# Two score slots and one probability slot in PSUM instead of three slots in rotation

## Chip, cores and metric

The kernel runs on one core of one Trainium2 chip. The metric is device time in microseconds, of the whole launch. Before the change three runs gave 754.0 us in the median (752.06 to 757.2).

## The reference

Input `x` is 4 batches of 1024 tokens with 128 channels. Cut to what matters, the computation for each batch is

```
k_eff, v_eff = products of W_dq, W_uq, W_uk, W_uv, W_o      # per head, 16 heads of 8 channels
c_kv  = x @ W_dkv.T ;  q = x @ W_dq.T @ W_uq.T
attn  = softmax(causal(q_lat @ c_kv.T / sqrt(8)))           # 1024 x 1024, 16 heads
y     = (attn @ c_kv) @ v_eff
x     = layernorm(x + y)
gate, up = fp4_linear(x, w_gate), fp4_linear(x, w_up)       # 128 -> 352, FP4 in blocks of 16
x     = layernorm(x + fp4_linear(silu(gate) * up, w_down))  # 352 -> 128
```

All in float32. The softmax subtracts the maximum of each query's row, and the kernel computes this maximum exactly, in a pass of its own.

## The kernel before, in words

**Tiling.** The heads go in four quads of four heads (`QUADS`), each quad in 18 steps (`STEPS`), so a batch has 72 steps (`BODY`) and the four batches 288. In each step TensorE computes two tiles of 128 x 1024 float32, each of which takes two banks of PSUM.

- A *score tile* S (`score_max`, lines 511 to 524) has queries on partitions. VectorE reads it for the maximum over the keys (`maximum`, line 837). It runs 24 steps (`STEPS + LEAD`) ahead of the other pass, and the first 24 tiles are made in a prologue. The maxima are combined after a quad's 18 tiles (line 846), split into three bf16 parts by GpSimd (`top_split`, lines 1080 to 1088), transposed by TensorE (`mt`, line 461), copied by ScalarE (line 686), and written by SyncE's DMAs as three more rows into the query operand (line 371).
- A *probability tile* T (`score_probs`, lines 526 to 542) has keys on partitions and subtracts the maximum through these rows. ScalarE reads it with one exp (`exps`, line 715) into `probs`, a ring of six buffers in SBUF.

Twelve times in 18 steps (`W_STEP`) TensorE multiplies finished probabilities by the values (`weigh`, line 556, called W here). Tiles that cross the causal diagonal get their mask as small matmuls (line 507).

**Where a tile lies.** PSUM has eight banks: `ring[0]` to `ring[2]` are three slots of two banks, `yt_ps` and `misc` one bank each. In the main loop the order of tiles S(0), T(0), S(1), T(1) and so on goes round the three slots: S(n) lies in slot 2n mod 3, T(n) in slot (2n+1) mod 3.

**What TensorE waits for.** Step n on TensorE is S(n), the jobs of the step, T(n), then W if there is one, in this order. S(n) overwrites the slot of T(n-2), so it waits for exp n-2. T(n) overwrites the slot of S(n-1), so it waits for the maximum of S(n-1). In the prologue S(s) waits for the maximum of S(s-3). In the last 24 steps of the last batch there are no more score tiles, and T goes round all three slots alone.

**The order of everything else** is written out by hand in `jobs` and in the tables `H_A`, `H_V`, `H_P`, `LN_AT`: for each step, which pieces of the projections, of the first norm and of the previous batch's feed-forward part run on which engine (`misc_job` on TensorE, `misc_read` and `sigmoid` on ScalarE, and so on). Each engine runs its own list in order. ScalarE's list for a step is its reads of `misc`, then the sigmoid of the feed-forward part (lines 722 and 724, behind GpSimd's clamp, line 1151), then the exp. After the last batch a tail does the feed-forward part of batch 3.

Of the kernel before, what the change touches and what calls it, by code (L numbers as in the profile page):

```python
# [30 lines left out]
LEAD = 6  # L31
STEPS = 18
P_RING = 6
# [16 lines left out]
def build(nc, x, w_dq, w_uq, w_dkv, w_uk, w_uv, w_o, w_gate, w_up, w_down, out):  # L50
    B, T, C = x.shape
# [96 lines left out]
    with ExitStack() as ctx:  # L148
# [168 lines left out]

        block = ctx.enter_context(nc.Block())

        def tile_pos(b, a, s):  # L320

            u = a + s // STEPS
            return b + u // QUADS, u % QUADS, s % STEPS
# [93 lines left out]
        def _(pe):  # L417
# [93 lines left out]
            def score_max(b, a, s, slot):  # L511

                if s == 0:
                    pe.wait_ge(op_in[a].sem, op_in[a].at(b, 3))
                for i, kc, p, at, n in S_LIST[s]:
                    pair = PAIRS * a + p
                    diag = kc == i // PER
                    for e in range(2):
                        lo = HALF * e
                        last = nc.tensor.matmul(ring[slot][:, e, at:at + n], q_op[lo:lo + ROWS, pair, i * P:(i + 1) * P],  # L520
                                                k_op[lo:lo + ROWS, pair, kc * CHUNK:kc * CHUNK + n], start=True, stop=not diag)
                    if diag:
                        last = causal(slot, at + n - P, mask_s)
                last.then_inc(s_mm.sem, 1)
# [53 lines left out]
                    nc.tensor.transpose(misc[0:w, 0:P], wd[:, f * P:f * P + w], ident[:, :]).then_inc(prep_mm.sem, 1)  # L578

            for s in range(STEPS + LEAD):  # L580
                if s >= 3:
                    pe.wait_ge(s_max.sem, s - 2)
                score_max(0, s // STEPS, s % STEPS, s % 3)
                if 4 <= s < 4 + 3 * FT:
                    weight_t(s - 4)
                if s == STEPS + 1:
                    pe.wait_ge(prep_cp.sem, 4 + 3 * FT)
                    misc_job("mt", 0, 0)
# [3 lines left out]
            for b in range(B + 1):  # L592
                if b == B:

                    pe.wait_ge(t_exp.sem, t_exp.at(B - 1, BODY - 1))
                for n in range(BODY):
                    if b < B:
                        a, s = n // STEPS, n % STEPS
                        nb, na, ns = tile_pos(b, a, s + STEPS + LEAD)
                        if nb < B:  # L600
                            if n < 2 and b == 0:
                                pe.wait_ge(s_max.sem, STEPS + LEAD)
                            else:
                                pn = b * BODY + n - 2
                                pe.wait_ge(t_exp.sem, pn + 1)
                            score_max(nb, na, ns, 2 * n % 3)
                    for job in jobs_at(b, n):
                        misc_job(*job)
                    if b < B:

                        if nb < B:
                            pe.wait_ge(s_max.sem, b * BODY + n + STEPS + LEAD)
                        else:
                            pe.wait_ge(s_max.sem, B * BODY)
                            pe.wait_ge(t_exp.sem, b * BODY + n - 2)
                        score_probs(b, a, s, (2 * n + 1) % 3)

                    for w, at in enumerate(W_STEP):
                        g = n - at
                        if g % STEPS == 0 and g >= 0 and b < B:  # L620
                            weigh(b, g // STEPS, w)
                        elif g % STEPS == 0 and g < 0 and b > 0:
                            weigh(b - 1, QUADS - 1, w)
# [3 lines left out]
        def _(act):  # L627
# [79 lines left out]
            def exps(b, a, s):  # L707

                n = STEPS * a + s
                act.wait_ge(t_mm.sem, t_mm.at(b, n))  # L710
                g = b * BODY + n - P_RING
                if g >= 0:

                    act.wait_ge(av_mm.sem, g // STEPS * WS + FREED[g % STEPS])
                nc.scalar.activation(probs[:, n % P_RING, :, :], ring[(2 * n + 1) % 3][:, :, :],  # L715
                                     ACT.Exp, scale=SCALE).then_inc(t_exp.sem, 1)

            def sigmoid(b, t):
# [76 lines left out]
        def _(dve):  # L795
# [34 lines left out]
            def maximum(b, a, s, slot):  # L830

                g = b * BODY + STEPS * a + s
                dve.wait_ge(s_mm.sem, g + 1)
                if s == 0 and g > 0:
                    dve.wait_ge(m_all.sem, b * QUADS + a)
                for i, kc, p, at, n in S_LIST[s]:
                    last = nc.vector.tensor_reduce(top[:, kc, :, p, i], ring[slot][:, :, at:at + n], AX.X, ALU.max)  # L837
                last.then_inc(s_max.sem, 1)
# [20 lines left out]
            dve.wait_ge(wq_v.sem, 3)  # L859
            nc.vector.tensor_scalar(w_b[:, :, :], w_b[:, :, :], 1.0, ROUND, ALU.max, ALU.mult).then_inc(wq_v.sem, 1)  # L860
            for s in range(STEPS + LEAD):
                maximum(0, s // STEPS, s % STEPS, s % 3)
                if s == STEPS - 1:
                    combine(0, 0)

# [122 lines left out]
            for b in range(B + 1):  # L988
                for n in range(BODY):
                    a, s = n // STEPS, n % STEPS  # L990
                    if b < B:
                        nb, na, ns = tile_pos(b, a, s + STEPS + LEAD)
                        if nb < B:
                            maximum(nb, na, ns, 2 * n % 3)
                            if ns == STEPS - 1:
                                combine(nb, na)
                    for kind, jb, k in jobs_at(b, n):
                        if kind == "k":
                            k_range(jb, k)
                        elif kind == "q":  # L1000
                            part_rest(jb, 2 + k)
                        elif kind == "yn":
                            output(jb, k)
                        elif kind == "up":
                            up_product(jb, k)
                        elif kind == "down" and k % 2:
                            second_sum(jb, k // 2)
                    if n in K_REST_AT and b + 1 < B:
                        part_rest(b + 1, K_REST_AT.index(n))
                    for nb, c, stage in first_norm_at(b, n):  # L1010
                        if stage == 0:
                            norm_stats(nb, c)
                        elif stage == 1:
                            first_norm(nb, c)
                        else:
                            quant_x(nb, c, stage - 2)
                    if b > 0:
                        for stage, t in tile_at(b, n, H_V if b < B else TAIL_H_V):
                            quant_h(b - 1, t, stage)
                        for c, stage in second_norm_at(b, n):  # L1020
                            (second_stats, last_norm)[stage](b - 1, c)
# [198 lines left out]
```

## Time and profile before

| | |
|---|---|
| median of 3 runs | 754.0 us (752.06 to 757.2) |
| profiled execution, its own time | 758.44 us |
| its span, first to last instruction | 756.6 us |
| TensorE matmul busy | 563.6 us (74%), 5863 instructions |
| VectorE busy | 532.3 us (70%), 981 |
| ScalarE busy | 412.3 us (54%), 598 |
| GpSimd busy | 316.0 us (42%), 441 |
| mean granted TensorE clock | 0.876 of full speed |

PE is TensorE's matmul, PEld its weight load, DVE VectorE, ACT ScalarE, POOL GpSimd, SPq SyncE's queue. A wait is the idle time of an engine ahead of an instruction, and the arrow names what released it. Busy time of an engine is a share over a prologue, a main loop and a tail that have different limits.

### The profile page before, as it was taken

What the parts mean: (1) busy time and instruction counts of PE and PEld (TensorE: products, weight loads), DVE (VectorE), ACT (ScalarE), POOL (GpSimd) and SP (SyncE); (2) the same over time, 40 slices, a digit from 0 to 9 for tenths busy, and PEclk for the clock granted to TensorE, in tenths of its full rate; (3) what the DMA queues carried; (4) which work ended last, traced back from release to release, by engine and by line L of the source; (5) the groups of instructions that cost most, each with busy time, mean ns of one, the idle gap of its engine ahead of it and who ended that gap; (6) DMA issues with size and microseconds to landing.
All of it is one profiled execution on the core that took longest, in us unless ns stands there. A gap on an engine that the chain in (4) does not pass through costs nothing.

```text
span 756.6 us, 15168 instructions
## 1 busy us (share of the span) xinstructions
PE 563.6 (74%) x5863; PEld 254.3 (34%) x5863; DVE 532.3 (70%) x981; ACT 412.3 (54%) x598; POOL 316.0 (42%) x441
## 2 busy tenths in 40 slices
PE   4275988589787888788888889696978897862623
PEld 2132333233333434333333334242323342421412
DVE  0389787388889767788788778888787784264461
ACT  2311766377665766565576666564656675742220
POOL 4520032000436654433337464533273536258682
PEclk9655999799998999999898999998899998995565
DMA  3393006602300192020300480203000000000000
GB/s 101 77 241 101 2 3 151 145 2 51 94 5 12 31 210 56 15 52 16 92 16 2 90 196 11 56 10 78 3 16 3 3 2 16 1 15 0 0 14 15
DMA packets 34222, 37.91 MB, mean 50 GB/s; under 512 B 6390, under 2 KB 19766, under 8 KB 34150
## 3 DMA queue, kind: packets, MB, share of 16 engines
q1 hardware_dynamic: 33238, 36.39, 20.0%
q8 instruction: 47, 0.77, 0.4%
q10 hardware_dynamic: 912, 0.54, 0.3%
q14 instruction: 25, 0.20, 0.1%
HBM read 19.64 MB, written 16.78 MB: 48 GB/s over the span
## 4 chain that ended last, share of the span: by engine, by line
PE 39%; DVE 31%; POOL 13%; issue 10%; ACT 4%; DMA 2%; SPq 1%; POOLq 0%; DVEq 0%; ACTq 0%
DVE top L837 19%; PE yt_ps L556 11%; PE ring L537 6%; PE ring L520 5%; PE misc L495 3%; PE ring L507 2%; PE misc L466 2%; POOL eg L1151 2%; POOL hx L1123 2%; POOL hx L1121 2%; POOL hx L1125 1%; DVE z L906 1%; PE misc L455 1%; PE misc L486 1%; DVE hc L963 1%
## 5 line engine op out<-in xcount | busy, mean ns | idle before, releaser
L837 DVE TENSOR_REDUCE top<-ring 128x2 f32<-128x1024 f32 (+3 forms) x384 | 349.6, 948 | 113.4 <-PE ring L507 80.2
L715 ACT ACTIVATE probs<-ring 128x1024 f32<-128x1024 f32 x288 | 293.8, 1027 | 132.1 <-PE ring L507 79.7
L556 PE MATMUL yt_ps<-probs,v_op 128*32 128x512 f32 (+3 forms) x1536 | 171.6, 520 | 0.5 <-ACT probs L715 0.5
L537 PE MATMUL ring<-q_op,k_op 59*128 59x512 bf16 (+3 forms) x768 | 124.0, 346 | 50.2 <-DVE top L837 40.3
L520 PE MATMUL ring<-k_op,q_op 56*128 56x512 f16 (+3 forms) x768 | 127.8, 355 | 44.5 <-ACT probs L715 18.9
L520 PEld LDWEIGHTS ring<-k_op,q_op 56*128 56x128 bf16 x768 | 38.4, 96 | 171.0 <-issue 116.8
L1144 POOL TENSOR_TENSOR r<-r,yq 128x128 f32<-128x128 f32 x32 | 14.6, 457 | 168.3 <-DVE yq L876 168.3
L537 PEld LDWEIGHTS ring<-q_op,k_op 59*128 59x128 f16 x768 | 37.7, 95 | 120.8 <-DVE top L837 58.7
L507 PE MATMUL ring<-ident,mask_s 64*128 64x64 bf16 x1024 | 59.5, 198 | 0.0
L507 PEld LDWEIGHTS ring<-ident,mask_s 64*128 64x128 bf16 x1024 | 47.7, 102 | 17.7 <-issue 5.0
L507 PEld LDWEIGHTS ring<-ident,mask_t 64*128 64x128 bf16 x1024 | 47.2, 100 | 18.2 <-issue 6.8
L507 PE MATMUL ring<-ident,mask_t 64*128 64x64 bf16 x1024 | 52.0, 196 | 0.0
L1151 POOL TENSOR_SCALAR eg<-eg 128x352 f32<-128x352 f32 x32 | 35.1, 1098 | 28.0 <-ACT eg L698 27.6
L722 ACT ACTIVATE eg<-eg,one 128x352 f32<-128x352 f32 x32 | 18.7, 586 | 41.0 <-POOL eg L1151 41.0
L556 PEld LDWEIGHTS yt_ps<-probs,v_op 128*32 128x32 f32 x1536 | 30.9, 110 | 29.6 <-issue 18.5
L1121 POOL TENSOR_TENSOR hx<-hx,hc 128x352 f32<-128x352 f32 x32 | 29.8, 931 | 20.7 <-DVE hc L966 20.7
L486 PE MATMUL ring<-ident,hx 128*128 128x128 f32 (+1 forms) x24 | 6.7, 414 | 42.6 <-POOL hx L1125 42.6
L1080 POOL TENSOR_SCALAR top_parts<-top_all 128x32 bf16<-128x32 f32 x16 | 4.8, 297 | 68.3 <-DVE top_all L846 68.2
L1123 POOL TENSOR_TENSOR hx<-hx,hc 128x352 f32<-128x352 f32 x32 | 29.8, 930 | 2.5
L1155 POOL TENSOR_TENSOR h<-gu,eg 128x352 f32<-128x352 f32 x32 | 29.8, 930 | 0.0
L963 DVE TENSOR_SCALAR hc<-hx 128x352 uint32<-128x352 uint32 x32 | 15.8, 492 | 16.3 <-POOL hx L1160 16.3
L1125 POOL TENSOR_TENSOR hx<-hx,h_sc 128x352 f32<-128x352 f32 x32 | 25.2, 787 | 2.5
(170 smaller groups left out, 758.4 us busy)
## 6 DMA issues: line engine op xcount, KB each, us to landing
q_op<-scratch_q SPq DMA_DIRECT2D x32, 224.0 KB
k_op<-scratch_k SPq DMA_DIRECT2D x32, 224.0 KB
scratch_k<-k_part SPq DMA_DIRECT2D x32, 192.0 KB, 3.3
scratch_q<-q_part SPq DMA_DIRECT2D x32, 128.0 KB, 3.1
scratch_q<-q_part SPq DMA_DIRECT2D x16, 192.0 KB, 3.3
xp<-in_L_attn_x_dram SPq DMA_DIRECT2D x4, 512.0 KB, 4.4
r<-in_L_attn_x_dram SPq DMA_DIRECT2D x8, 256.0 KB, 2.8
out_dram<-z SPq DMA_DIRECT2D x8, 256.0 KB, 2.3
```

Source lines behind the costliest of these rows:

```text
L507: last = nc.tensor.matmul(ring[slot][:, e, at + HALF * half:at + HALF * (half + 1)], mask[group, half, :], ident16[group, group], start=Fa ...
L520: last = nc.tensor.matmul(ring[slot][:, e, at:at + n], q_op[lo:lo + ROWS, pair, i * P:(i + 1) * P], k_op[lo:lo + ROWS, pair, kc * CHUNK:kc ...
L537: last = nc.tensor.matmul(ring[slot][:, e, at:at + n], k_op[lo:lo + rows, pair, j * P:(j + 1) * P], q_op[lo:lo + rows, pair, (c + 1) * CHU ...
L556: last = nc.tensor.matmul(yt_ps[32 * q:32 * (q + 1), lo:CHUNK], v_op[:, j, 4 * a + q, :], probs[:, (STEPS * a + tile) % P_RING, q % 2, at: ...
L715: nc.scalar.activation(probs[:, n % P_RING, :, :], ring[(2 * n + 1) % 3][:, :, :], ACT.Exp, scale=SCALE).then_inc(t_exp.sem, 1)
L837: last = nc.vector.tensor_reduce(top[:, kc, :, p, i], ring[slot][:, :, at:at + n], AX.X, ALU.max)
L963: nc.vector.tensor_scalar(hc[:, n, :, :].bitcast(U32), hx[:, n, :, :].bitcast(U32), 0x7F800000, None, ALU.bitwise_and).then_inc(he_v.sem, 1)
L1121: nc.gpsimd.tensor_tensor(dst, dst, magic, ALU.add).then_inc(s1.sem, 1)
L1123: nc.gpsimd.tensor_tensor(dst, dst, magic, ALU.subtract).then_inc(s2.sem, 1)
L1125: nc.gpsimd.tensor_tensor(dst, dst, sc_, ALU.mult).then_inc(s3.sem, 1)
L1151: nc.gpsimd.tensor_scalar(eg[:, n, :], eg[:, n, :], EXP_TOP, None, ALU.min).then_inc(e_p.sem, 1)
L1155: nc.gpsimd.tensor_tensor(hn.rearrange("p n k -> p (n k)"), gu[:, n, :], eg[:, n, :], ALU.mult).then_inc(h_p.sem, 1)
```

## The change

The slots get fixed owners. In the main loop score tiles take slots 0 and 1 in turn (n mod 2), and probability tiles always take slot 2, up to the last 24 steps, where T goes round all three as before. The waits follow: S(n) waits for the maximum of S(n-2), T(n) for exp n-1. In the prologue score tiles also use two slots, so S(s) waits for the maximum of S(s-2). No operation on data is added, removed or moved in any engine's order.

```diff
@@ -317,6 +317,10 @@
 
         block = ctx.enter_context(nc.Block())
 
+        def probs_slot(m):
+
+            return 2 if m < B * BODY - STEPS - LEAD else m % 3
+
         def tile_pos(b, a, s):
 
             u = a + s // STEPS
@@ -578,9 +582,9 @@
                     nc.tensor.transpose(misc[0:w, 0:P], wd[:, f * P:f * P + w], ident[:, :]).then_inc(prep_mm.sem, 1)
 
             for s in range(STEPS + LEAD):
-                if s >= 3:
-                    pe.wait_ge(s_max.sem, s - 2)
-                score_max(0, s // STEPS, s % STEPS, s % 3)
+                if s >= 2:
+                    pe.wait_ge(s_max.sem, s - 1)
+                score_max(0, s // STEPS, s % STEPS, s % 2)
                 if 4 <= s < 4 + 3 * FT:
                     weight_t(s - 4)
                 if s == STEPS + 1:
@@ -598,22 +602,19 @@
                         a, s = n // STEPS, n % STEPS
                         nb, na, ns = tile_pos(b, a, s + STEPS + LEAD)
                         if nb < B:
-                            if n < 2 and b == 0:
-                                pe.wait_ge(s_max.sem, STEPS + LEAD)
-                            else:
-                                pn = b * BODY + n - 2
-                                pe.wait_ge(t_exp.sem, pn + 1)
-                            score_max(nb, na, ns, 2 * n % 3)
+                            pe.wait_ge(s_max.sem, b * BODY + n + STEPS + LEAD - 1)
+                            score_max(nb, na, ns, n % 2)
                     for job in jobs_at(b, n):
                         misc_job(*job)
                     if b < B:
 
                         if nb < B:
-                            pe.wait_ge(s_max.sem, b * BODY + n + STEPS + LEAD)
+                            if b * BODY + n > 0:
+                                pe.wait_ge(t_exp.sem, b * BODY + n)
                         else:
                             pe.wait_ge(s_max.sem, B * BODY)
                             pe.wait_ge(t_exp.sem, b * BODY + n - 2)
-                        score_probs(b, a, s, (2 * n + 1) % 3)
+                        score_probs(b, a, s, probs_slot(b * BODY + n))
 
                     for w, at in enumerate(W_STEP):
                         g = n - at
@@ -712,7 +713,7 @@
                 if g >= 0:
 
                     act.wait_ge(av_mm.sem, g // STEPS * WS + FREED[g % STEPS])
-                nc.scalar.activation(probs[:, n % P_RING, :, :], ring[(2 * n + 1) % 3][:, :, :],
+                nc.scalar.activation(probs[:, n % P_RING, :, :], ring[probs_slot(b * BODY + n)][:, :, :],
                                      ACT.Exp, scale=SCALE).then_inc(t_exp.sem, 1)
 
             def sigmoid(b, t):
@@ -859,7 +860,7 @@
             dve.wait_ge(wq_v.sem, 3)
             nc.vector.tensor_scalar(w_b[:, :, :], w_b[:, :, :], 1.0, ROUND, ALU.max, ALU.mult).then_inc(wq_v.sem, 1)
             for s in range(STEPS + LEAD):
-                maximum(0, s // STEPS, s % STEPS, s % 3)
+                maximum(0, s // STEPS, s % STEPS, s % 2)
                 if s == STEPS - 1:
                     combine(0, 0)
 
@@ -991,7 +992,7 @@
                     if b < B:
                         nb, na, ns = tile_pos(b, a, s + STEPS + LEAD)
                         if nb < B:
-                            maximum(nb, na, ns, 2 * n % 3)
+                            maximum(nb, na, ns, n % 2)
                             if ns == STEPS - 1:
                                 combine(nb, na)
                     for kind, jb, k in jobs_at(b, n):
```

## Rows read from the trace of the kernel before

**Rows 1.** The page: the chain that ended last, by engine.

```profile
PE 39%; DVE 31%; POOL 13%; issue 10%; ACT 4%; DMA 2%; SPq 1%; POOLq 0%; DVEq 0%; ACTq 0%
```

**Rows 2.** Busy us by stretch, then granted clock and DMA share.

```profile
72.00:630.00 558.00, 463.80 (x5187) 200.52 (x5187) 443.27 (x785) 351.05 (x479) 217.57 (x313) 0.94 0.21 49
...
666.00:757.00 91.00, 35.89 (x140) 23.72 (x132) 41.25 (x106) 21.34 (x52) 54.86 (x62) 0.60 0.03 9
```

**Rows 3.** TensorE waits, 72 to 630 us: line, releaser, total us, times, longest.

```profile
PE ring L537 <- DVE top L837: 40.3, 47, 2.6
PE ring L520 <- ACT probs L715: 18.9, 13, 2.4
...
PE misc L451 <- DVE gu L939: 7.7, 6, 3.0
PE misc L474 <- DVE yq L876: 3.1, 3, 1.2
PE misc L461 <- POOL top_parts L1088: 2.9, 9, 0.5
PE misc L455 <- DVE rest L828: 2.7, 4, 1.0
PE misc L480 <- DVE yq L876: 1.7, 3, 0.6
PE misc L486 <- POOL hx L1125: 1.4, 5, 0.3
PE misc L495 <- DVE gu L939: 1.1, 3, 0.4
```

**Rows 4.** Waits of VectorE, 72 to 630 us.

```profile
DVE top L837 <- PE ring L507: 72.0, 64, 9.8
DVE top L837 <- PE ring L520: 31.7, 40, 2.7
```

**Rows 5.** Waits of ScalarE, 72 to 630 us.

```profile
ACT eg L722 <- POOL eg L1151: 19.6, 11, 3.1
```

**Rows 6.** Line 715: count, ns min/median/max, first and last start, 72 to 630 us.

```profile
L715 ACT ACTIVATE probs<-ring x264: 1003/1024/1061, 71.7 to 628.5; 128x1024 f32<-128x1024 f32 x132
```

**Rows 7.** Line 537, 72 to 630 us, the same columns.

```profile
L537 PE MATMUL ring<-q_op,k_op x702: 216/376/631, 72.5 to 629.5; 59*128 59x512 bf16 x89, 59*128 59x128 bf16 x58, 59*128 59x256 bf16 x29
```

**Rows 8.** TensorE timeline: start, us, operation, [idle before <- releaser], 311 to 334 us.

```profile
311.95 0.39 PE L537 MATMUL ring<-q_op,k_op 59*128 59x512 bf16 x2
...
315.72 0.39 PE L537 MATMUL ring<-q_op,k_op 59*128 59x512 bf16 x2
...
318.58 0.28 PE L520 MATMUL ring<-k_op,q_op 56*128 56x256 f16 x2 [2.41 <-ACT probs L715]
...
330.05 0.39 PE L537 MATMUL ring<-q_op,k_op 59*128 59x512 bf16 x2 [1.08 <-DVE top L837]
...
333.17 0.34 PE L537 MATMUL ring<-q_op,k_op 59*128 59x384 bf16 x2
```

**Rows 9.** ScalarE timeline, 311 to 337 us.

```profile
312.38 1.02 ACT L715 ACTIVATE probs<-ring 128x1024 f32<-128x1024 f32 x1 [1.08 <-PE ring L537]
...
317.52 1.01 ACT L715 ACTIVATE probs<-ring 128x1024 f32<-128x1024 f32 x1
...
328.21 1.02 ACT L715 ACTIVATE probs<-ring 128x1024 f32<-128x1024 f32 x1 [0.56 <-PE ring L507]
...
332.42 1.02 ACT L715 ACTIVATE probs<-ring 128x1024 f32<-128x1024 f32 x1
```

**Rows 10.** Timeline of the prologue, 40 to 75 us.

```profile
41.58 20.85 DVE L837 TENSOR_REDUCE top<-ring 128x2 f32<-128x1024 f32 x24 [7.65 <-PE ring L507]
...
65.24 3.75 SPq L371 DMA_DIRECT2D q_op<-top_t  x6
...
70.54 0.61 PE L520 MATMUL ring<-k_op,q_op 56*128 56x512 f16 x2 [2.88 <-DVE top L837]
```

**Rows 11.** DMA issues, 60 to 75 us: count, KB each, median us to landing.

```profile
q_op<-top_t SPq DMA_DIRECT2D x6, 4.0 KB, 1.7
```

## What the change will do to the time

> **What bounds the kernel now.** I read the busy time by stretch first [rows 2]. After a prologue comes the main loop, and from 666 us on a tail that has no S or T tile. Between 72 and 630 us, where both kinds of tile run, TensorE is busy for 463.8 of 558 us (83%), VectorE for 443.3 (79%), ScalarE for 351.1 (63%). So TensorE is the spine of the loop, with VectorE close behind, and the chain that ended last says the same: PE 39%, DVE 31%, ACT 4% [rows 1]. No engine is full. What counts is therefore how TensorE's idle time, 94.2 us = 558 - 463.8, is made up.
>
> The waits of TensorE in this stretch give the answer [rows 3]. T tiles waited 40.3 us for VectorE's maximum (47 times), S tiles 18.9 us for the exp (13 times), and the jobs in `misc` waited for other work, 20.6 us over the seven rows shown (7.7 + 3.1 + 2.9 + 2.7 + 1.7 + 1.4 + 1.1). The first two, 59.2 us, are exactly the waits for a free slot that the change takes away. VectorE in turn waited 103.7 us (72.0 + 31.7) for score tiles [rows 4], so it could take them earlier: it doesn't stop a gain by itself.
>
> **What the change takes away.** T(n) no longer waits for the maximum of S(n-1). S(n) no longer waits for exp n-2. At most 59.2 us come back. The new wait of S(n), for the maximum of S(n-2), lies one tile of VectorE's work earlier than what T(n) waited for, and TensorE has T and W in between, so I cost it at nothing. What hides it is VectorE being done by then. That cover shrinks when TensorE gets ahead, and the price if it goes is in the rivals.
>
> **What it adds.** T(n) now waits for exp n-1, which is the reader of the tile just before it. The chain T, exp, T has one slot and can't overlap with itself. Its floor comes from two rows: T starts at 311.95 [rows 8], its exp at 312.38 and takes 1.02 us [rows 9], so it ends 1.45 us after the T started. From the end of a releaser to the matmul it releases there are 0.05 to 0.06 us (exp 317.52 + 1.01 = 318.53, S tile 318.58). The floor is 1.51 us from T to T, and somewhat more for a masked T. The mean interval of the loop is 555.6 / 262 = 2.12 us, well above it. But the intervals are very uneven, since W and the jobs come in some steps only: the waiting T has W(n-1), S(n) and the jobs of n as its cover, and without W and job that is one S tile. Behind the waiting T on TensorE's queue are W(n), S(n+1) and all later jobs; for W and for S waits VectorE and `yt_ps`, so a late T delays everything but the exp itself.
>
> **How I worked out the sum.** There are 264 exps in the loop, the first at 71.7 and the last at 628.5 us [rows 6], and T matmuls from 72.5 to 629.5 us [rows 7]. For each of the 262 intervals from the second T to the 264th I took the old length, subtracted the idle time that a removed wait had caused in it, and compared this with the time from the T's start to its exp's end, plus 0.06. The larger is the new length. Where the exp was late only since ScalarE had a backlog from the exp before, I counted ScalarE's own work between the two exps instead. That is because a T that waits for the exp before it lets no backlog of exps build up. Three examples:
> - T at 330.05 waited 1.08 us for VectorE [rows 8]. The exp before it ended at 328.21 + 1.02 = 329.23 [rows 9]. The T moves up to 329.29, so 0.76 us come back, not 1.08.
> - T at 333.17 had no wait [rows 8]. The exp before it ends at 332.42 + 1.02 = 333.44 [rows 9]. The T moves back to 333.50: 0.33 us lost.
> - T at 315.72 had no wait [rows 8]. The exp before it ended only at 318.53 [rows 9], since ScalarE stood behind a sigmoid that waited for GpSimd's clamp: such waits are 19.6 us, 11 times, in the loop [rows 5]. The T moves to 318.59, 2.87 us later. But the S tile at 318.58 had waited 2.41 us for that same exp [rows 8], and that wait goes. What stays is the T tile's own time, which used to run beside the stall: about 0.4 us. So most of the 18.9 us of S waits is no gain. The stall moves one tile up.
>
> For two quads in full: from 287.2 us the changes are +0.48, +0.33, +0.14, +0.32, +0.02, +2.86 - 2.48, +0.14, together +1.8 us. The next one, from 327.7 us, has more waits for VectorE: -0.02, -0.76, +0.33, +0.08, -0.32, +0.38, +0.32, +1.01, -0.20, -0.72, -0.66, -0.16, together -0.7 us. Over all 262 intervals 103 get longer by 45.5 us and 39 shorter by 33.5 us. **The main loop's term is +12.0 us.**
>
> The other terms: the last 24 steps keep their waits (T for exp n-3) and the tail has no ring at all, 0. In the prologue VectorE runs without a pause, 18 tiles in 24 instructions and 20.85 us, 1.16 us a tile, while a score tile without a mask takes TensorE 0.61 us (70.54) [rows 10]. So the second slot is filled while VectorE reads the first. The first S tile of the main loop may start one tile earlier than at 70.54, which is worth at most 1.2 us to VectorE. T(0) behind it gains almost nothing, since its maximum rows come from six DMAs whose issue ends at 65.24 + 3.75 = 68.99, plus 1.7 to landing [rows 11]: 70.7. I take 0, with bounds of -1.2 and, for a maximum that now and then finds its tile late, +2.
>
> Sum: 0 + 12 + 0 = +12 on the profiled execution's 758.4, so 770. The median of the runs is 754.0, 4.4 us under the profiled execution. I carry the difference over and get 766. The sum leaves two corrections of opposite sign open (the jobs' waits, which can swallow delays, and gains that VectorE doesn't let through). The first seems to me a little surer, as each job wait lies right behind some T: I take 2 us off. **764 us**, 1.3% slower.
>
> A page of the Trainium skill speaks against this change outright: Perfetto Trace Analysis, section Matmuls, wants independent matmul groups to rotate through different PSUM banks so that the reading of one overlaps the next group's matmuls, and the T tiles stop doing so. The rows bear this out in part only, as 159 of the 262 intervals (262 - 103) don't get longer. Taken as a rule without exception it would keep the losses and none of the gains, 754 + 45.5 = 799; that is the far end of the second rival.
>
> **The rivals.**
> 1. *The delays are swallowed (faster).* The jobs of a step sit right behind a late T or just ahead of the next one, and they waited 20.6 us in the rows for VectorE and GpSimd [rows 3]. A T that comes late ahead of such a job costs nothing. If all of it is swallowed, and the prologue's 1.2 us come too: 12 - 20.6 - 1.2 = -9.8, so 744 us. It decides from the point where more than 12 of these 20.6 us fall into intervals that got longer. For it: 59.2 us of slot waits go for certain, and VectorE has 103.7 us in which it waits for TensorE [rows 4]. Against it: the job waits are few (the 7.7 us are six waits), and 103 delays are spread over all steps.
> 2. *The lockstep costs more (clearly slower).* The gains of 33.5 us need S(n+1) to go out early, and it now waits for the maximum of S(n-1) in its turn. VectorE is 79% busy. If half of the gains stay with VectorE: 12 + 16.8 = 29, so 783 us. If none comes: 799. For it: in the quad from 327.7 us the T waits for VectorE follow each other closely. Against it: VectorE's idle time.
> 3. *It evens out (no change).* The 59.2 us of removed waits meet new waits of the same size, with half of the job waits swallowed: 12 - 10.3 = +1.7, so 756 us.
> 4. *It stays on paper.* If TensorE were the bound at nearly every step, neither wait would matter. Its 94.2 us of idle time speak against that, so I give it no chance of its own and put it into the third.
>
> **How the numbers follow.** Forecast (758 to 772 us) 0.41, second rival 0.16, third 0.22, first 0.21. A measurement of this kernel tells about 1% from no change, 746.5 to 761.5 us. The first rival's chance goes to faster, 0.20, with the little that is left near the edge. Of the forecast's own chance some 0.07 lies below 761.5, so same is 0.30, and slower 0.50. The range takes in rival 1's price and rival 2's half price: 743 to 784. Outside it remain a swallowing larger than the rows show, and the upper end of rival 2.
>
> **What would show it in the changed profile.**
> - TensorE's wait of line 537 for VectorE (40.3 us now) gone, and in its place one for ScalarE's exp, of some 50 to 60 us.
> - Its wait of line 520 for the exp (18.9) gone. A new one of line 520 for VectorE below 10 us would confirm my zero for it, and one of 20 or more would be rival 2.
> - No interval from T to T under 1.5 us. At the step where ScalarE waits for GpSimd's clamp the stall of 2.4 us stands ahead of the T, not of the S.
> - VectorE's waits for score tiles up by about 10 us, with its busy time the same.
> - Job waits on TensorE: near 20 us by my sum, near 0 by rival 1.
>
> I'm wrong if the exp has more cover than its end times say, if the order of work on ScalarE comes out differently once T tiles are late, or if a late T makes a maximum late and through it the chain of max, split, transpose and DMA that opens each quad: that would come 15 times, and nothing above prices it.

## The result: 3.0% slower

| | before | changed |
|---|---|---|
| median | 755.6 us (4 runs) | 779.0 us (4 runs) |
| ratio | | 1.030 [1.026, 1.034] |
| profiled execution, its span | 758.4, 756.6 us | 778.2, 776.4 us |
| T(1) to T(263) | 555.6 us | 576.3 us |

The forecast was slower, 764 us; measured is 779. The direction was right, the amount less than half of what came: +10 forecast, +23.4 measured. 779 lies within the range and near the half price of the second rival (783). Two executions took twice the usual time, 1733 us in e1 and 1563 us in one of the kernel before, and are left out of every comparison.

Of the changed kernel first the chain by engine and the busy time by stretch, with the columns of [rows 1, 2]. The loop ends 20 us later, so the stretches do too.

```profile
PE 40%; DVE 19%; ACT 14%; POOL 12%; issue 10%; DMA 2%; SPq 1%; POOLq 0%; ACTq 0%; DVEq 0%
```

```profile
72.00:650.00 578.00, 472.42 (x5177) 201.82 (x5177) 440.90 (x784) 353.66 (x478) 216.82 (x312) 0.93 0.20 47
...
686.00:777.00 91.00, 35.50 (x136) 23.83 (x132) 40.23 (x106) 21.19 (x52) 54.53 (x62) 0.62 0.03 9
```

ScalarE's share of the chain went from 4% to 14%, VectorE's from 31% to 19%. All of the loss lies in the main loop. Prologue and tail are the same. In this stretch TensorE idles for 105.6 us (578 - 472.4) in place of 94.2, and is busy for 472.4 us in place of 463.8. The sum had no term for the second; the section on the prediction takes it up. Now its waits in the loop, as in [rows 3], then VectorE's and ScalarE's, as in [rows 4, 5].

```profile
PE ring L541 <- ACT probs L716: 68.6, 96, 2.8
PE ring L541 <- issue: 9.7, 2, 7.9
PE ring L524 <- DVE top L838: 6.6, 4, 3.1
PE misc L455 <- DVE gu L940: 5.5, 6, 1.9
PE misc L459 <- DVE rest L829: 3.4, 6, 0.6
PE misc L478 <- DVE yq L877: 3.2, 3, 1.1
PE misc L465 <- POOL top_parts L1089: 2.2, 5, 1.2
PE ring L541 <- DVE top L838: 1.1, 1, 1.1
```

```profile
DVE top L838 <- PE ring L511: 86.3, 69, 8.8
DVE top L838 <- PE ring L524: 39.9, 40, 2.6
```

```profile
ACT eg L723 <- POOL eg L1152: 21.3, 11, 3.1
```

Line 541 is T (537 before), line 524 is S (520), line 716 the exp, line 838 the maximum. The waits of 40.3 and 18.9 us are gone. T waits 68.6 us for the exp, 96 times. VectorE waits 126.2 us for score tiles (86.3 + 39.9), where it waited 103.7.

The three examples of the prediction can be read in two views of the changed kernel, TensorE's timeline and ScalarE's:

```profile
328.51 0.39 PE L541 MATMUL ring<-q_op,k_op 59*128 59x512 bf16 x2 [2.79 <-ACT probs L716]
...
339.34 0.39 PE L541 MATMUL ring<-q_op,k_op 59*128 59x512 bf16 x2 [0.32 <-ACT probs L716]
...
342.79 0.34 PE L541 MATMUL ring<-q_op,k_op 59*128 59x384 bf16 x2 [0.26 <-ACT probs L716]
...
347.73 0.39 PE L541 MATMUL ring<-q_op,k_op 59*128 59x512 bf16 x2
...
349.24 0.39 PE L541 MATMUL ring<-q_op,k_op 59*128 59x512 bf16 x2 [0.44 <-ACT probs L716]
```

```profile
326.43 0.59 ACT L723 ACTIVATE eg<-eg,one 128x352 f32<-128x352 f32 x1 [3.08 <-POOL eg L1152]
...
327.45 1.01 ACT L716 ACTIVATE probs<-ring 128x1024 f32<-128x1024 f32 x1
```

The T at 315.72 in [rows 8] is now at 328.51, behind the sigmoid's stall and the exp that ends at 328.46. The T at 330.05 there waits 0.32 us in place of 1.08, now for the exp. The T at 333.17, which didn't wait, waits 0.26. From 347.73 to 349.24 one sees the floor, 1.51 us. Over the loop no interval is shorter than 1.50 us; before, 60 were under it.

### The profile page after: what moved, and what is told of

The parts are those of the page before. It is cut to its first block, busy times and chain, and to the rows that moved or that the text cites. A ratio compares the mean times of both kernels' runs of the same rounds, so it can differ in the third digit from the quotient of the medians.

```text
span 776.4 us, 15168 instructions
## 1 busy us (share of the span) xinstructions
PE 572.4 (74%) x5863; PEld 255.5 (33%) x5863; DVE 530.2 (68%) x981; ACT 415.6 (54%) x598; POOL 315.3 (41%) x441
## 3 DMA queue, kind: packets, MB, share of 16 engines
q1 hardware_dynamic: 33238, 36.39, 19.6%
## 4 chain that ended last, share of the span: by engine, by line
PE 40%; DVE 19%; ACT 14%; POOL 12%; issue 10%; DMA 2%; SPq 1%; POOLq 0%; ACTq 0%; DVEq 0%
PE yt_ps L560 13%; DVE top L838 10%; ACT probs L716 10%; PE ring L541 8%; PE ring L524 5%; PE misc L499 3%; POOL eg L1152 3%; PE ring L511 3%; PE misc L484 1%; DVE z L907 1%; POOL hx L1124 1%; POOL hx L1122 1%; ACT yt L732 1%; ACT eg L723 1%; PE misc L490 1%
## 5 line engine op out<-in xcount | busy, mean ns | idle before, releaser
L541 PE MATMUL ring<-q_op,k_op 59*128 59x512 bf16 (+3 forms) x768 | 124.9, 348 | 81.1 <-ACT probs L716 68.6
L560 PE MATMUL yt_ps<-probs,v_op 128*32 128x512 f32 (+3 forms) x1536 | 173.9, 526 | 0.5 <-ACT probs L716 0.5
L524 PE MATMUL ring<-k_op,q_op 56*128 56x512 f16 (+3 forms) x768 | 129.7, 359 | 31.8 <-DMA k_op<-scratch_k 18.0
```

What stands on the lines that cost most here:

```text
L541: last = nc.tensor.matmul(ring[slot][:, e, at:at + n], k_op[lo:lo + rows, pair, j * P:(j + 1) * P], q_op[lo:lo + rows, pair, (c + 1) * CHU ...
L560: last = nc.tensor.matmul(yt_ps[32 * q:32 * (q + 1), lo:CHUNK], v_op[:, j, 4 * a + q, :], probs[:, (STEPS * a + tile) % P_RING, q % 2, at: ...
```

## The experiments

Two theories were left after the result. **Lockstep**: the loss is T's wait for the exp of the tile before it. **VectorE**: VectorE holds back the S tiles, which now have two slots, and with them the gains. And one question: what the removed waits gave back. Ratios are to the kernel before, with their 95% intervals.

**A short maximum (e1, e2, e11).**

```
-  nc.vector.tensor_reduce(top[...], ring[slot][:, :, at:at + n], AX.X, ALU.max)
+  nc.vector.tensor_reduce(top[...], ring[slot][:, :, at:at + n // 8], AX.X, ALU.max)
```

The exp's scale is also multiplied by 0.01 here, in this pair and in e12, so that nothing overflows. The length of the exp stays at 1.03 us.

> The kernel before, with VectorE's row maximum over an eighth of each tile's columns (and the exp's scale times 0.01, so that nothing overflows; both change the values). Theory: before the change the T tiles wait 40.3 us for VectorE; with a short maximum that wait falls below 3 us and TensorE gets most of it back, so 715 to 735 us. Rival (VectorE's load limits both kernels alike, and the change lost by what S tiles wait for VectorE): the same fall here, and an equal one in the changed kernel.

> The changed kernel with the same short maximum. Theory: its loss is T waiting for the exp of the tile before, which VectorE has no part in. So T's wait for ScalarE stays at 60 us or more, S's wait for VectorE goes from 6.6 to 0, and the time falls by 5 to 12 us only, to 767 to 774: the distance to the kernel before grows from 23 to 40 us or more. Rival (the gains are held back by VectorE): it falls by 30 or more, and the distance stays at 23 or shrinks.

> The same kernel as e1, for a profile of an undisturbed execution: 700 to 704 us, T's wait for VectorE below 3 us, TensorE busy above 85% between 72 and 600 us.

Measured: before with it 702.7 us, 0.929 [0.925, 0.933]; changed with it 744.0 us, 0.986 [0.983, 0.989]. e11 is e1's kernel again, for its trace; its one run gave 705.9 us. The distance grows from 23 to 41 us, with VectorE busy for 278 us in place of 532 (e11, whole span). TensorE's waits for slots, first in e11, then in e2 (72 to 650 us):

```profile
PE ring L520 <- ACT probs L715: 16.7, 15, 2.2
PE ring L537 <- DVE top L837: 6.0, 5, 2.7
```

```profile
PE ring L541 <- ACT probs L716: 61.6, 100, 1.8
```

T's wait for the exp stays at 61.6 us when VectorE is quick, and the distance grows, so VectorE is not what makes the changed kernel slower than the other. But I had the changed kernel falling by 5 to 12 us, and it fell by 35, which was one of the two marks that I had set for the rival. So VectorE's length counts there too, although its rows have few waits for the maximum (6.6 and 1.1 us). Of the 30 us between T(1) and T(263), 19.3 are idle time of TensorE and 10.8 busy time with the same matmuls (472.0 to 461.2), and its clock was at the lower level for 52 us there in place of 76. What of VectorE's work sets the pace, no run here separates.

**A short exp (e3, e4).**

```
-  nc.scalar.activation(probs[:, n % P_RING, :, :], ring[...][:, :, :], ACT.Exp, ...)
+  w = CHUNK if b == 0 and n < P_RING else CHUNK // 2
+  nc.scalar.activation(probs[:, n % P_RING, :, 0:w], ring[...][:, :, 0:w], ACT.Exp, ...)
```

> The kernel before, with the exp over half of each tile's columns, from the seventh tile on (the other half of the probabilities stays as it was). Exp from 1.03 to about 0.6 us. Theory: T's wait for VectorE stays at about 40 us and S's wait for the exp falls little, since it comes from the clamp of the feed-forward part: 745 to 754 us. Rival: ScalarE's length counts before too, below 740.

> The changed kernel with the same short exp. Theory: the floor from T to T falls from 1.51 to about 1.08 us, so T's wait for the exp falls from 68.6 to 20 to 30 us (what stays is the clamp's stall), and the kernel is level with the one before with the same exp or up to 20 us faster: 730 to 755 us. Rival (something else in the fixed slots costs, whatever the exp's length): it stays 15 us or more slower than the kernel before with the same exp.

Measured: before with it 748.7 us, 0.991 [0.988, 0.995]; changed with it 749.2 us, 0.993 [0.990, 0.996]. **The 3% is gone.** In e4 the exp takes 0.60 us, T's wait for it is 35.6 us and S's wait for VectorE 12.5 us (72 to 650 us):

```profile
PE ring L541 <- ACT probs L717: 35.6, 48, 2.4
PE ring L524 <- DVE top L839: 12.5, 14, 3.2
```

The shortest interval there is 1.075 us, as the floor less 0.43 says. The exp's length is what makes the fixed slots slow. Note the second row, though: with the exp out of the way, S waits for VectorE about twice as long as in the changed kernel (6.6 us). The fixed slots are level with the rotation and not faster.

**The new wait alone (e5, e17), and the price of a second semaphore (e16, e18).** e5 and e17 are one kernel, the one before with

```
+  if nb < B and b * BODY + n > 0:
+      pe.wait_ge(t_exp.sem, b * BODY + n)
   score_probs(b, a, s, (2 * n + 1) % 3)
```

> The kernel before with its three slots in rotation, and one more wait: T(n) also waits for exp n-1, which no slot asks for. It has the changed kernel's new wait and keeps the two old ones, so it splits the change: up to here it's what the new wait costs, and from here to the changed kernel what the removed waits give back. Worked out interval by interval from the trace of before, as in the prediction but with T's waits for VectorE kept: +28.6 us, so 780 to 786 us, 3 to 10 us slower than the changed kernel. Rival (the slots' places in PSUM or the two-slot prologue cost something, not the wait): close to 754.

Measured 786.6 us, 1.040 [1.036, 1.044]. On the face of it the new wait costs 30 us and the removed ones give back 7.6. But its trace has 263 instructions more, the second waits. A T that waits for the exp comes 0.14 us after the exp's end, not 0.055, and the shortest interval is 1.59 us, not 1.50. The experiment had a cost of its own. The same kernel with the short maximum on top, where T's wait for VectorE is down to 4.6 us, shows it:

> The kernel with rotation and T's extra wait for exp n-1 (as the kernel of both waits), with the row maximum over an eighth of the columns and the exp's scale times 0.01. With a short maximum VectorE holds no T tile back, so the two waits that the change removes are worth nothing, and the fixed slots give nothing back: within 4 us of the changed kernel with the short maximum, 740 to 748 us. If it is 8 or more slower, the fixed slots give back something that isn't a wait for VectorE.

Measured 753.7 us, 0.998 [0.995, 1.001], where the changed kernel had 744.0 with the short maximum: 10 us more. So I ran controls. In the first the changed kernel gets a second wait that is always fulfilled (`pe.wait_ge(s_max.sem, b * BODY + n + STEPS + LEAD - 1)` ahead of the one for the exp), in the last the kernel before does (`pe.wait_ge(t_exp.sem, b * BODY + n - 1)`).

> The changed kernel, whose T tile also waits once more for the maximum of S(n-2), which its own S(n) has waited for already: a wait that is always fulfilled. It's the control for the kernel of both waits: there a T tile waits for two semaphores, and in its trace the T comes 0.10 us after the exp's end in place of 0.055, with a shortest interval of 1.59 us in place of 1.50. If the second wait by itself costs that 0.05 to 0.09 us at each of some 110 T tiles that wait, this kernel is 5 to 10 us slower than the changed one, 784 to 789, and level with both waits: then the removed waits give back nothing, and the new wait alone costs about 20. If it stays at 779, the new wait costs 30 and the removed ones give back 7.

> The kernel of both waits, for a comparison on the same chip with the spare wait: 783 to 788 us. The difference to the spare wait's kernel is what the removed waits are worth, with the number of waits on each T equal.

> The kernel before, whose T tile also waits for exp n-2, which its own S(n) has waited for already. A second wait that is always fulfilled: it should cost only where T is the tile that TensorE gets stuck at, 47 times, so 0 to 5 us: 754 to 760. If it costs 8 or more, two semaphores on a matmul slow the stream everywhere.

The 0.10 us in the text on e16 is a misreading: in e5's trace, of which it speaks, 112 of 113 such tiles have 0.14 to 0.15 us, and in e16 114 of 115 have 0.143. The 0.09 us of the intervals is right.

| | us | ratio |
|---|---|---|
| changed kernel | 779.0 | 1.030 [1.026, 1.034] |
| changed, spare wait (e16) | 786.8 | 1.040 [1.036, 1.044] |
| both waits (e17) | 785.9 | 1.039 [1.035, 1.042] |
| before, spare wait (e18) | 755.3 | 0.999 [0.996, 1.001] |

e16 and e17 have the same number of waits on each T. e17 has the two old slot waits, and e16 doesn't; they also differ in the slots themselves and in the prologue's two or three. They are level: on one chip e17 is 0.9 us faster, each ratio known to 0.4%. **The removed waits give back nothing that can be measured**, which here means less than about 4 us. In the traces, between T(1) and T(263), TensorE idles for some 2 us less in e16 (110.2, against 112.5 in e17) and is busy for 5 us more (472.3, against 467.2). The second wait costs the changed kernel 1.0%, some 8 us. The 4% of e17 less this 1% leaves the whole 3% to the new wait; that is a difference of two runs, not a run of its own.

In e18 the second wait costs nothing, although T tiles are waited for there too: 51 of them start 0.056 us after the maximum's end, as before (0.057). The traces show what differs. In the kernels with two waits (e5, e16, e17, e18) T's first weight load carries the wait for the maximum, and the wait for the exp is an instruction of its own ahead of it. The T tiles of e17 that the maximum released start 0.057 us behind it (14 of them), those that the exp released 0.143 us behind it (116). So what costs is that the wait that ends last is the separate instruction. e16's exp and the T behind it:

```profile
287.04 1.02 ACT L717 ACTIVATE probs<-ring 128x1024 f32<-128x1024 f32 x1 [1.08 <-PE ring L541]
...
288.21 0.39 PE L541 MATMUL ring<-q_op,k_op 59*128 59x512 bf16 x2 [0.93 <-ACT probs L717]
```

TensorE's waits for VectorE and ScalarE in e17 show why little comes back (72 to 650 us):

```profile
PE ring L537 <- ACT probs L717: 75.0, 107, 2.9
PE ring L537 <- DVE top L839: 11.8, 14, 1.6
```

The waits for the maximum are all still in force here, and yet they are 11.8 us in place of 40.3. The wait for the exp comes first and VectorE catches up behind it.

**The sigmoid one step later (e6, e7).** `H_A = (2,)` becomes `H_A = (3,)`.

> The kernel before, with ScalarE's sigmoid of the feed-forward part one step later in its list (H_A from 2 to 3), so that the exp of the step goes ahead of it and doesn't stand behind GpSimd's clamp. S's wait for the exp (18.9 us) falls below 5, ScalarE's wait for the clamp (19.6) below 8: 740 to 750 us. Rival (the stall moves on, to the jobs that need the product behind the sigmoid): within 4 us of 754.

> The changed kernel with the same later sigmoid. Its stall of 2.4 to 2.9 us stands ahead of T, eight times. T's wait for the exp falls from 68.6 to 45 to 52 us and the time from 779 by 8 to 16 us, to 763 to 771. The distance to the kernel before with the same edit stays at 18 to 24, since by the prediction's sum the stall only changed its place. If the distance falls below 12, the stall was a good part of what the change costs.

Measured: before with it 760.0 us, 1.005 [1.003, 1.007]; changed with it 773.3 us, 1.023 [1.021, 1.026]. I was wrong on the first: S's wait for the exp fell to 4.9 us as expected, and the kernel got slower. The time went into the job behind it (e6, 72 to 650 us):

```profile
PE misc L486 <- POOL hx L1125: 17.5, 6, 3.2
...
PE ring L520 <- ACT probs L715: 4.9, 9, 1.2
```

Before, that job waited 1.4 us for GpSimd [rows 3]. The S tile's wait had run beside GpSimd's work. In the changed kernel T's wait for the exp fell by 19 us, to 49.3, and the kernel got only 6 us faster, since the same job waits there too (e7, 72 to 650 us):

```profile
PE ring L541 <- ACT probs L716: 49.3, 86, 1.6
PE misc L490 <- POOL hx L1126: 14.7, 7, 2.9
```

The distance is 13 us, so the edit brings the two kernels closer by 10 us. My sum had 3.7 us for the stall (+16.5 and -12.8 at steps 13 and 14). The 10 us are no measure of it, as some 4 of them are what the kernel before lost by the edit; the 6 us of the changed kernel are nearer.

**One slot for S, two for T (e8).** `probs_slot` returns `1 + m % 2`, `score_max` uses slot 0, the prologue three slots, and the waits follow.

> The mirror of the change: score tiles in one slot and probability tiles in two, in turn (the prologue with three slots, as before the change). S(n) then waits for the maximum of S(n-1), T(n) for exp n-2. In the trace of before 164 of 264 S tiles start before that maximum ends, by 128 us together, with VectorE's other work between two maxima. Much worse than the change, then: 820 to 870 us. Rival (two slots for T are worth more than two for S): below 779.

Measured 807.2 us, 1.068 [1.065, 1.072]. That is less than the 820 to 870 that I said, but the worst of the three ways to share the slots. S waits where T waited (72 to 650 us):

```profile
PE ring L524 <- DVE top L838: 102.0, 144, 1.8
```

**Slots by a plan (e9, e10).** Both use one function that keeps the occupant of each slot and waits for that occupant's reader; a list `OTHER` names the tiles that don't take the oldest slot.

```
+  for m in range(B * BODY):
+      for kind in ("ST" if m < BUSY else "T"):
+          k = order[OTHER.get((kind, m), 0)]
+          order.remove(k)
+          order.append(k)
+          SLOT[kind, m], HELD[kind, m] = k, held[k]
+          held[k] = (kind, m)
```

> The kernel before, except that in eleven quads the S tile of step 14 takes the slot of the S tile of step 13 in place of the slot of the T tile of step 12, whose exp is the one that stands behind the clamp. T of step 14 takes that one. S's wait for the exp falls from 18.9 us to below 5 and T's wait for it appears with 5 to 12 us. About -6 us: 745 to 751. Rival (as in the later sigmoid, the stall moves on with nothing gained): within 2 us of the kernel before.

> Three slots, each tile taking the one whose reader ended first in the trace of before: 30 T tiles take the slot of the last T, 14 S tiles that of another than the oldest tile, all others the oldest as before. So it has the changed kernel's removed waits where they were real and its new wait almost nowhere. T's wait for VectorE falls from 40 to 10 us or less, S's wait for the exp to below 5, T's wait for the exp stays below 15. If the removed waits come back in full where no lockstep takes them: about -16 us, 736 to 742. If VectorE holds them back (the S tile behind waits for the same maximum in its place): -6 to -9, 745 to 749, and S's wait for VectorE goes up to 8 us or more.

Measured: e9 753.4 us, 0.995 [0.992, 0.998]; e10 754.0 us, 0.994 [0.991, 0.998], 12 runs each. In e9 S's wait for the exp fell from 18.9 to 3.2 us, and the job's wait for `hx` rose from 1.4 to 13.4. Both are faster than the kernel before by half a percent by their ratios, 4 us, not by the 16 that the removed waits would be worth. In e10 (72 to 650 us):

```profile
PE ring L558 <- DVE top L850: 18.6, 32, 1.9
PE misc L507 <- POOL hx L1138: 13.5, 7, 3.2
...
PE ring L541 <- DVE top L850: 8.6, 15, 1.0
...
PE ring L558 <- ACT probs L728: 7.2, 14, 0.9
PE misc L482 <- POOL top_parts L1101: 5.7, 10, 2.0
PE ring L541 <- ACT probs L728: 4.9, 8, 1.0
```

Waits for a slot are 39.3 us (18.6 + 8.6 + 7.2 + 4.9) in place of 59.2. The job waits for `hx` and `top_parts` are 19.2 in place of 4.3. So 20 us went and 15 came back one instruction later. In the timeline it is plain. Where S waited 2.41 us for the exp before [rows 8], e10 has

```profile
316.35 0.28 PE L541 MATMUL ring<-k_op,q_op 56*128 56x256 f16 x2 [0.69 <-DVE top L850]
...
318.86 0.87 PE L507 MATMUL misc<-ident,hx 128*128 128x128 f32 x3 [2.00 <-POOL hx L1138]
```

**The job behind the removed wait, one step later (e13, e14, e15).** `(20 + 6 * t, "ht", -1, t)` becomes `(21 + 6 * t, ...)`.

> The kernel before, with the transposition of the feed-forward part's quantized tile (ht) one step later in all lists, 21 + 6t in place of 20 + 6t. Before the change the S tile of step 14 waits 2.4 us for an exp just ahead of that job, which so finds its input ready (1.4 us of waits in all). One step later it is ready all the more: within 3 us of 754. Rival (the feed-forward chain itself is late): 745 or less, or 760 and more.

> The planned slots with ht one step later. There the job's wait for GpSimd was 13.5 us, where it was 1.4 before: it took over the time of the S tile's removed wait. If that was what swallowed the gain, its wait falls below 6 us and the time by 4 to 9 us, to 743 to 749. If it doesn't fall, the removed waits were no time at all at these places, since GpSimd's and VectorE's own chain sets the pace.

> The changed kernel with ht one step later. There the stall for the clamp stands ahead of T of step 13, so ht finds its input ready (0 in the waits): within 3 us of 779. It is the control for the planned kernel: if it gets faster by 4 us or more, the later ht is good by itself.

Measured: before with it 785.1 us, 1.043 [1.039, 1.047]; planned 786.4 us, 1.044 [1.040, 1.048]; changed 817.3 us, 1.085 [1.081, 1.089]. All three lose about 4 to 5%, so the test failed as a test of where the 15 us went. The new place costs by itself: the job now waits for the read of `misc` by the job before it, and ScalarE, ahead of its exp, for the job (e13, 72 to 640 us, TensorE, then ScalarE).

```profile
PE misc L486 <- DVE yq L876: 20.4, 12, 2.7
```

```profile
ACT h_t L704 <- PE misc L486: 38.0, 20, 3.5
```

Planned slots and rotation are level here (786.4 and 785.1 us).

## Why the prediction had the direction and not the size

**The floor: right.** 1.51 us from T to T was forecast, 1.50 is the shortest interval and 1.51 the plain one. I had 103 longer intervals, and 105 got longer (by more than 0.05 us). T's wait for the exp was forecast at 50 to 60 us and is 68.6. The short exp shows that the exp's length, and through it this wait, is the cause of the 3%.

**The prologue: right.** T(0) starts 0.7 us earlier, against 0 with bounds of -1.2 and +2.

**The stall at step 13: moved as forecast, priced slightly low.** The intervals of steps 13 and 14 changed by +16.5 and -11.6 us, where the sum had +16.5 and -12.8: 4.9 us net, not 3.7. Taking most of the stall away gave the changed kernel 6 us (e7).

**The main loop's term: this step failed.** The sum had +12.0 us, and T(1) to T(263) took 20.8 us longer. 105 intervals got longer by 61.9 us and 57 shorter by 41.4, where the sum had 45.5 and 33.5. Two steps of it were wrong.

*TensorE's own time was put at no change, without a reason.* The sum says that an interval less the idle time of a removed wait is what TensorE needs. Here are the busy times between T(1) and T(263), before and changed, with the columns of [rows 2]. Both kernels run the same 5173 matmuls in the same order.

```profile
72.47:628.05 555.59, 462.63 (x5173) 200.03 (x5175) 440.89 (x781) 349.56 (x478) 217.38 (x312) 0.94 0.21 48
```

```profile
72.05:648.40 576.35, 471.91 (x5173) 201.63 (x5175) 439.28 (x780) 352.63 (x477) 216.82 (x312) 0.93 0.20 47
```

Idle time grew by 11.5 us (92.96 to 104.44), against the sum's +12.0. The other 9.3 us are busy time (462.63 to 471.91). Compared matmul by matmul they come in three parts. 4450 matmuls ran at the full clock in both kernels. Their own durations add up to nearly the same (1472.5 and 1473.7 us), but they overlap less, as TensorE starts from idle 165 times in place of 132: 4.3 us. The matmuls that ran at the lower level (1.2 GHz) in one of the kernels only add 3.9 us net, those at the lower level in both 1.0. The clock was at that level for 62.4 us of this stretch before and for 76.1 us in the changed kernel. One interval shows it, T(158) to T(159), with no wait in either kernel, first before (from 394.36 to 397.10), then changed (from 405.78 to 410.84). In the changed kernel TensorE had just stood 1.56 us for the exp ahead of T(157), and the clock was at its lower level from 404.2 to 411.0 us:

```profile
394.73 1.06 PE L556 MATMUL yt_ps<-probs,v_op 128*32 128x512 f32 x8
...
396.04 1.12 PE L451 MATMUL misc<-x_t,bk 128*128 128x512 f32 x2
```

```profile
406.43 1.93 PE L560 MATMUL yt_ps<-probs,v_op 128*32 128x512 f32 x8
...
408.83 2.08 PE L455 MATMUL misc<-x_t,bk 128*128 128x512 f32 x2
```

The mean granted clock of the changed kernel's four runs is 0.869, that of the kernel before 0.878 to 0.881 on the chips where it ran several times. Whether the fixed slots bring this about, and how, no run here separates.

*What the removed waits give back was priced too high.* By the same sum the kernel of both waits came to +28.6 us, so these waits were worth 16.6 (28.6 - 12.0). e16 and e17 show nothing that can be measured. The traces show two reasons. First, VectorE catches up behind the new wait: with both in force T's wait for it falls from 40.3 to 11.8 us by itself (e17). Second, the same release is asked for again by the next instruction. T(144) waited 2.56 us for the maximum of S(143) before the change:

```profile
364.06 0.61 PE L537 MATMUL ring<-q_op,k_op 59*128 59x512 bf16 x2 [2.56 <-DVE top L837]
```

In the changed kernel it doesn't, and S(145) right behind it waits 3.14 us for the same maximum:

```profile
370.72 0.38 PE L541 MATMUL ring<-q_op,k_op 59*128 59x512 bf16 x2
...
374.65 0.29 PE L524 MATMUL ring<-k_op,q_op 56*128 56x128 f16 x2 [3.14 <-DVE top L838]
```

The interval to T(144) got 2.51 us shorter and the one after it 2.70 longer. The sum had the first and not the second. I costed S's new wait at nothing because it is due "one tile of VectorE's work earlier", and forgot that the wait of S(n+1) is for the very tile T(n) used to wait for. That sentence was in the second rival, with 16%. Such waits of S are 6.6 us in all, at four tiles, so they are a part of the miss only. The largest misses are two quads: +4.2 and +3.6 us in place of -0.9 and +0.5. Of the +4.2 us 2.5 are busy time, of the +3.6 only 0.5.

That the idle time alone came out as forecast is partly luck. An estimate from e17, e16 and the changed kernel: idle time grew by 19.6 us with both waits, of which 5.8 go with the second semaphore (110.2 - 104.4). That leaves about 14 for the new wait, where the sum had 28.6, and about 2 for the removed ones, where it had 16.6. The two errors cancel.

**The correction of -2 us: wrong sign.** I took job waits to swallow delays. Those seven rows did fall, from 20.6 to 15.6 us (5.5 + 3.4 + 3.2 + 2.2, and 1.3 in two rows under 1 us), but the time behind the sum went up and not down.

**My own check would have misled.** "Line 520 for VectorE below 10 us confirms my zero": it is 6.6 us, and the zero was still wrong, since such a wait undoes a gain that T had one tile earlier. VectorE's waits for score tiles were to go up by about 10 us and went up by 22.5.

**The rest.** The profiled executions differ by 19.8 us, the medians by 23.4. The one of before was 2.8 us above its median, the one of the changed kernel 0.8 below. That is within the spread of the runs (752 to 760 and 773 to 782).

The page of the Trainium skill that spoke against the change, Perfetto Trace Analysis, section Matmuls (independent groups should rotate through different PSUM banks), was right for this kernel in its direction: T lost its rotation and the kernel 3%. The 799 us that I had worked out for the rule without exception weren't reached. The mirror (e8) adds what the rule leaves open: in this kernel the tiles read by VectorE, the busier of the two readers, lose more when they stop rotating (6.8%).

## What to carry to other kernels

A tile with a single slot is in lockstep with its reader; compare matmul plus reader with the shortest, not the mean, interval between two such tiles. A removed wait is worth nothing until you have asked what the next instructions on that engine wait for: follow the release, not the wait, and look for it one instruction later. A sum of idle time is only half of the change: compare the busy time of the same instructions too. When an experiment adds a wait, run a control with a wait that is always fulfilled, and see in the trace which of the two waits is an instruction of its own.

## What was unexpected in the hardware

- A second wait ahead of a matmul costs time when the one that ends last is the separate instruction: 0.143 us from the release to the matmul in place of 0.055, 0.09 us in the shortest interval, and 8 us over 115 such tiles (e16). Where the last wait is the one that the weight load carries, it costs nothing: 0.056 and 0.057 us at 51 tiles each with and without the second (e18 and before), and 0.999 in time.
- Planned slots removed idle time, and the granted clock fell. In the profiled executions it is 0.862 in place of 0.876; over all of e10's runs the mean is 0.870, over those of the kernel before on the same chip 0.878. Between T(1) and T(263) TensorE idles for 8.0 us less in e10 and is busy for 6.8 us more with the same matmuls. Of the stretch behind the 2.00 us wait of e10, here first e10 and then the kernel before (columns of [rows 2]):

```profile
317.00:330.00 13.00, 10.55 (x117) 4.09 (x117) 8.28 (x13) 8.00 (x12) 6.67 (x8) 0.74 0.18 43
```

```profile
317.00:330.00 13.00, 9.31 (x115) 3.69 (x115) 8.11 (x13) 8.22 (x12) 6.94 (x9) 0.87 0.19 42
```

Both kernels pause there, and the clock is at its lower level (1.2 GHz) for longer in e10, where matmuls are busy for 10.55 us with what takes 9.31 before. It takes another part of what the plan gave. Why the clock is lower over e10's runs wasn't tried.
